# Weight loads put behind row stores, and the start of the first attention sequence in another order, in a fused FFN, mLSTM and FFN kernel

## The reference

```python
x = x + 0.5 * moe_ffn(layernorm(x))    # 8 experts, one per token: relu(x @ w1[e] + b1[e]) @ w2[e] + b2[e], times its softmax share
x = x + attn(layernorm(x))             # gated linear attention (mLSTM), below
x = x + 0.5 * moe_ffn(layernorm(x))    # same weights as the first

def attn(x):                           # 8 heads of 64; hidden width 512, inner width 256
    xn = layernorm(x) * g + b
    x_t, r_t = xn @ W_up_l.T + b_up_l, xn @ W_up_r.T + b_up_r
    x_c = silu(causal_conv4_over_features(x_t))
    q, k, skip = (x_c @ W.T + b for W_q, W_k / 8, W_skip);  v = x_t @ W_v.T + b_v
    i, f = softcap(x_c @ W_i.T + b_i), softcap(x_c @ W_f.T + b_f);  o = sigmoid(x_t @ W_o.T + b_o)
    # scan over the 512 tokens with a state c[h] (64 x 64), its normalizer n[h] and a running maximum m[h]
    h = o * scan(q, k, v, i, f)
    return (head_layernorm(h) + skip) * silu(r_t) @ W_down.T + b_down + x
```

## Time and profile before

| | |
|---|---|
| median of three runs | 426.08 us |
| profiled execution, in all | 429.1 us |
| its span, first to last instruction | 427.3 us |
| TensorE busy | 375.8 us (88%) |
| VectorE busy | 316.3 us (74%) |
| ScalarE busy | 236.5 us (55%) |
| GpSimd busy | 122.1 us (29%) |
| mean granted clock of TensorE | 0.946 |

### The profile page before, as it was taken

How to read it: one execution, slowest core, us unless ns; L and a number is a source line. 1 busy time by engine, 2 the same in 40 slices (tenths; PEclk the granted TensorE clock), 3 DMA queues, 4 the chain that set the end, 5 groups by cost and what they waited for, 6 DMA issues and landing times.

```text
span 427.3 us, 11335 instructions
## 1 busy us (share of the span) xinstructions
PE 375.8 (88%) x3628; PEld 301.4 (71%) x3629; DVE 316.3 (74%) x1007; ACT 236.5 (55%) x634; POOL 122.1 (29%) x123
## 2 busy tenths in 40 slices
PE   8147999977999999999999999999989866879991
PEld 5117999723687787887878878778768733679990
DVE  7833777653658898878989788988789994658780
ACT  3734656611546767467684567655556912646550
POOL 2333543077001111103110120111031168334552
PEclk9566999996999999999999999999999989889997
DMA  7996223111799997876730000000002612323320
GB/s 171 392 316 237 68 71 59 38 43 44 151 179 188 187 176 184 180 181 153 185 92 0 0 0 0 0 0 0 2 2 60 228 62 83 117 69 90 98 67 1
DMA packets 57089, 44.57 MB, mean 104 GB/s; under 512 B 4063, under 2 KB 53857, under 8 KB 56673
## 3 DMA queue, kind: packets, MB, share of 16 engines
q1 hardware_dynamic: 54018, 38.14, 37.5%
q0 software_dynamic: 2752, 5.73, 4.8%
q10 hardware_dynamic: 288, 0.31, 0.4%
HBM read 17.98 MB, written 25.73 MB: 102 GB/s over the span
## 4 chain that ended last, share of the span: by engine, by line
PE 68%; ACT 9%; DVE 7%; issue 6%; DMA 4%; POOL 2%; another core or an unknown queue 1%; POOLq 0%; ACTq 0%; SPq 0%; DVEq 0%
PE bank L960 64%; ACT WVT L837 3%; DMA xn_rows<-XN 2%; POOL slots L531 2%; DMA XB<-xn_rows,IDX 1%; DVE ST L1508 1%; ACT XN L659 1%; PE bank L1086 1%; PE bank L1343 1%; ACT E L846 1%; ACT W1R L857 1%; DVE QS L2111 1%; PE bank L1244 1%; DMA XN<-slots 1%
## 5 line engine op out<-in xcount | busy, mean ns | idle before, releaser
L599 POOL TENSOR_TENSOR HS<-HS,MHALF 128x8 f32<-128x8 f32 x16 | 26.4, 1647 | 130.6 <-DVE HS L2161 130.6
L737 ACT ACTIVATE HT<-bank,W1R 128x128 f32<-128x128 f32 x138 | 40.6, 365 | 21.3 <-issue 11.0
L960 PE MATMUL bank<-XBT,W1R 128*128 128x128 f32 x368 | 51.9, 286 | 0.1
L960 PE MATMUL bank<-W,HT 128*128 x368 | 50.1, 280 | 0.5 <-issue 0.5
L960 PEld LDWEIGHTS bank<-XBT,W1R 128*128 128x128 f32 x368 | 47.2, 201 | 0.8 <-issue 0.4
L960 PEld LDWEIGHTS bank<-W,HT 128*128 128x128 f32 x368 | 46.1, 197 | 1.0 <-issue 0.7
L837 ACT ACTIVATE WVT<-bank,AC 128x128 f32<-128x128 f32 x128 | 36.5, 375 | 11.7 <-PE bank L960 11.3
L960 PE MATMUL bank<-MASKB,IDB 128*128 128x512 bf16 x111 | 35.7, 424 | 7.9 <-DVE CREDIT L1960 5.2
L801 ACT ACTIVATE QKT<-bank,COLS 128x512 f32<-128x512 f32 x32 | 22.0, 687 | 28.9 <-PE bank L960 28.9
L545 POOL DMA_INDIRECT XB<-xn_rows,IDX x23 | 22.6, 984 | 32.9 <-PE bank L1086 19.9
L584 POOL DMA_INDIRECT out<-YB,IDX x23 | 22.6, 983 | 25.8 <-DVE YB L1794 17.4
(11 more groups left out here) (377 smaller groups left out, 989.0 us busy)
## 6 DMA issues: line engine op xcount, KB each, us to landing
slots<-FILL SPq DMA_DIRECT2D x74, 258.0 KB
W<-w SPq DMA_DIRECT2D x2, 2048.0 KB, 12.3
XN<-slots SPq DMA_DIRECT2D x23, 129.0 KB
W<-w SPq DMA_DIRECT2D x1, 2064.0 KB, 7.9
y_rows<-YB SPq DMA_DIRECT2D x23, 64.0 KB
X<-x SPq DMA_DIRECT2D x4, 256.0 KB, 5.3
xn_rows<-XN SPq DMA_DIRECT2D x2, 512.0 KB, 8.8
XN<-X SPq DMA_DIRECT2D x1, 768.0 KB, 5.1
```

Of the source, the lines that this page charges most:

```text
L599: g.tensor_tensor(HS[:, 3, :], HS[:, 2, :], MHALF[:, 0:H], ALU.pow).then_inc(roots_ready, 1)
L737: ins = a.activation(HT[:, j % 2, c, :], bank[2 + j % 2][:, c * P:(c + 1) * P], ACT.Relu, bias=W1R[:, j % 2, F + c:F + c + 1])
L960: return t_.matmul(o, l, r, start=start, stop=stop, skip_group_check=True)
```

## The change

- **SP.** W1 waits for two quarters of X, not for four. W2 is loaded in two halves, one behind each store of `xn_rows`, and counted by a semaphore of its own (`w2_loaded`). The constants wait for the third transpose of a block. The attention weights are loaded one by one behind the y stores of blocks 0 to 6.
- **GpSimd.** After the first four gathers of y come both roots, and then the other twelve gathers; three of these twelve stood ahead of the roots.
- **ScalarE.** `cast_mask` moves from turn 1 of the blocks to the front of `split_weights`.
- **VectorE.** The setups after the first move back: softmax shares behind block 2, the others behind blocks 6, 8, ... 22. `folds_low` is taken apart: the low parts for W_up_r and W_v before `scale_norm`, the one for W_o behind it. `conv_low` now signals on `folds_split` too.
- **TensorE.** Ten products of ones are added between the ranks and the map. Before the first z, 8 + 9 products stand around the wait for the variance in place of 10 ahead of it and 7 behind the folds' wait. `head_z` and `head_x` wait only for `conv_low`; the wait for all low folds stands ahead of the v and o projections.

```diff
@@ SP
-            sp.wait_ge(x_loaded[3], 16)
+            sp.wait_ge(x_loaded[1], 16)
             sp.dma_start(W1[:, :, :], w1).then_inc(ffn_loaded, 16)
             sp.dma_start(B2[:, :, :], b2.partition_broadcast(P)).then_inc(ffn_loaded, 16)
-            sp.dma_start(W2[:, :, :, :], w2).then_inc(ffn_loaded, 16)
-            for lo, hi in GROUPS[0]:
+            for n, (lo, hi) in enumerate(GROUPS[0]):
                 sp.wait_ge(xn_ready[0], hi)
                 sp.dma_start(xn_rows[lo * P:hi * P, :].rearrange("(t p) d -> p t d", p=P), XN0[:, lo:hi, 0:D])\
                     .then_inc(rows_sent, 16)
+                half = slice(n * NE // 2, (n + 1) * NE // 2)
+                sp.dma_start(W2[:, half, :, :], w2[:, half, :, :]).then_inc(w2_loaded, 16)
+            sp.wait_ge(xbt_full[0], 3)
             sp.dma_start(COLS[:, :], colpack).then_inc(cols_loaded, 16)
...
+            store_block(0, 0)
+            sp.dma_start(WULT[:, :], wult).then_inc(folds_loaded, 16)
+            sp.dma_start(WURT[:, :], wurt).then_inc(folds_loaded, 16)
+            sp.dma_start(WIFT[:, :, :], wift).then_inc(folds_loaded, 16)
+            store_block(1, 1)
+            sp.dma_start(WVT[:, :, :], wvt).then_inc(folds_loaded, 16)
+            store_block(2, 2)
+            sp.dma_start(WOT[:, :, :], wot).then_inc(folds_loaded, 16)
...
+            store_block(6, 2)
+            sp.dma_start(WDT[:, :, :], wdt).then_inc(attn_loaded, 16)
@@ GpSimd, first_outputs
-                pool.wait_ge(fold_full, 4)
-                to_tokens(range(4, 7), y_loaded[4])
                 pool.wait_ge(cols_loaded, 48)
                 norms(0)
-                to_tokens(range(7, 8), y_loaded[4])
+                pool.wait_ge(fold_full, 4)
+                to_tokens(range(4, 8), y_loaded[4])
@@ ScalarE: out of turn 1 of the first FFN, and into split_weights
                 act.wait_ge(y_full[0], NBLK)
+                cast_mask()
                 act.wait_ge(attn_consts, 1)
@@ TensorE, first FFN
+                    for n in range(10):
+                        mm(bank[7][:, :], MASKB[:, 0:P], MASKB[:, :])
                     pe.wait_ge(high_ready, 2)
...
-                pe.wait_ge(ffn_loaded, 48)
-                if f == 1:
-                    pe.wait_ge(w2_loaded, 16)
+                pe.wait_ge(ffn_loaded, 32)
+                pe.wait_ge(w2_loaded, 48 if f else 32)
@@ TensorE, start of the attention
             spin(4, 0)
             pe.wait_ge(y_loaded[3], 16)
-            spin(10, 0)
+            spin(8, 0)
             pe.wait_ge(a_var, 1)
+            spin(9, 0)
             pe.wait_ge(folds_split, 1)
-            spin(7)
             head_z(0)
-            spin(3)
+            spin(3, 1)
             head_x(0)
+            pe.wait_ge(folds_split, 2)
             project(0, 0, "v")
@@ VectorE
-                        if k % 2 == 0 and k // 2 < len(setup):
-                            setup[k // 2]()
+                        if k == 2:
+                            setup[0]()
+                        elif k > 4 and k % 2 == 0:
+                            setup[k // 2 - 2]()
...
                 conv_low()
+                fold_low(WURL, WURH, 6)
+                fold_low(WVL, WVH, 7)
                 scale_norm(0)
-                folds_low()
+                fold_low(WOL, WOH, 4)
+                folds_done()
```

More of the change, by code:

```diff
@@ L429, in _, with store_block @@
                     .then_inc(rows_sent, 16)
+                half = slice(n * NE // 2, (n + 1) * NE // 2)
+                sp.dma_start(W2[:, half, :, :], w2[:, half, :, :]).then_inc(w2_loaded, 16)
+            def store_block(k, j):
+                sp.wait_ge(y_ready[0], k + 1)
+                sp.dma_start(y_rows[bass.ds(k * P, P), :], YB[:, j, :]).then_inc(y_sent[0][j], 16)
+            sp.wait_ge(xbt_full[0], 3)
             sp.dma_start(COLS[:, :], colpack).then_inc(cols_loaded, 16)
@@ L433, in _ @@
             sp.dma_start(K[:, FIRST:], consts[:, FIRST:KEPT]).then_inc(consts_loaded, 16)
[L434 to L438, removed]
-            def store_block(k, j):
-                sp.wait_ge(y_ready[0], k + 1)
-                sp.dma_start(y_rows[bass.ds(k * P, P), :], YB[:, j, :]).then_inc(y_sent[0][j], 16)
-            with sp.Fori(0, TAIL // RING) as n:
+            store_block(0, 0)
[6 more added lines that the diff above has]
+            sp.dma_start(WOT[:, :, :], wot).then_inc(folds_loaded, 16)
+            store_block(3, 3)
+            sp.dma_start(WQT[:, :, :], wqt).then_inc(attn_loaded, 16)
+            store_block(4, 0)
+            sp.dma_start(WKT[:, :, :], wkt).then_inc(attn_loaded, 16)
+            store_block(5, 1)
+            sp.dma_start(WSKT[:, :, :], wskt).then_inc(attn_loaded, 16)
+            store_block(6, 2)
+            sp.dma_start(WDT[:, :, :], wdt).then_inc(attn_loaded, 16)
+            store_block(7, 3)
+            with sp.Fori(2, TAIL // RING) as n:
                 for j in range(RING):
@@ L745, in turn @@
                         relu(k + 1, (j + 1) % RING)
-                    if f == 0 and isinstance(k, int) and k == 1:
-                        cast_mask()
                     if f == 1 and isinstance(k, int) and k + 3 < AHEAD:
@@ L1745, in first_route @@
                 dve.wait_ge(eid_ready[f], 1)
-                dve.wait_ge(ffn_loaded, 48)
+                dve.wait_ge(ffn_loaded, 32)
                 copy_w1(0, 0, 0)
@@ L1952, in conv_low, with fold_low, folds_done @@
                 step.settle()
[L1954 to L1958, removed]
+                v.memset(CREDIT[:, 9:10], 0.0).then_inc(folds_split, 1)
+            def fold_low(low, high, i):
+                dve.wait_ge(w_high, {6: 5, 7: 6, 4: 7}[i])
+                did(v.tensor_tensor(low[:, :], bank[i][:, :], high[:, :].bitcast(F32), ALU.subtract))
+            def folds_done():
                 step.settle()
```

## The result

The changed kernel took 423.91 us (median of 15 runs, 422.37 to 426.39) against 426.06 (15 runs) for the kernel before: ratio 0.995, 95% interval 0.9926 to 0.9975. Forecast was 413.0 with a range of 409.5 to 418.5. The sign was right, the size was not: 2.2 us came of 13.4. The profiled execution took 422.66 us, with a span of 420.7.

A forecast was written before the change was run, and what follows sets the result against it. The prediction took TensorE to bound the block loop, with the chain leaving it for gathers and the wait before z. It summed 6.2 + 1.2 + 0 + 6.0 = 13.4 us, from 426.08 to 413.0, range 409.5 to 418.5.

The forecast's parts named there:

- part 4: From the last block to the gates: earlier roots, z and x products gain 6.0 us, bounds 3.5 and 6.5.
- Everything after it keeps its spacing: Behind the first x bank's read, tanh, silu, 11 products and gates were to shift whole, keeping the 6.0 us gain.
- part 2: TensorE's clock in the first blocks: less time at half clock, gain 1.2 us, bounds 0 and 2.7.
- Part 1: First FFN until its blocks start: earlier stores and faster gathers gain 6.2 us, bounds 2.8 and 6.8.
- 2.7 us bound: Upper bound of the clock gain: the time lost while the first 5.36 us of the blocks run at 0.50.
- blocks run above 2.0 us: Sign in the first FFN's block loop that the forecast is wrong; blocks were expected to stay 1.90 us apart.
- Part 3: Weight loads beside the first FFN's blocks: forecast to cost 0, bounds 0 and 1.6 us.
- Slow gathers: Rival at the first gathers: they stay slow beside W2's last half, gain 10.0 us, time 416.1; chance 0.12.
- starved gathers: Rival at blocks 4 to 12: weight loads starve the block gathers, making the kernel slower, up to 430; chance 0.03.
- The clock did fall: Rival: the clock falls anyway in the first blocks and around z, gain 9.7 us, time 416.4; chance 0.13.

The follow-up runs named there:

- e1: An unchanged copy of the kernel before, measured and traced again: 426.35 us, ratio 0.997.
- e9: The changed kernel, with GpSimd waiting for the gates' products before the gathers of tiles 8 to 15: 422.49 us, ratio 0.990.
- e17: Changed kernel, only GpSimd reordered: block gathers 3 to 6 one a block; three token gathers ahead of the roots, five behind, four after the gates: 418.71 us, ratio 0.981.
- e13: As e9, but in the blocks GpSimd runs three gathers ahead of the transposes instead of four: 421.52 us, ratio 0.990.
- e10: As e9, with the weight loads, the tables and the setups that need them moved later in the blocks: 421.84 us, ratio 0.988.
- e16: As e3, with the block gathers three ahead instead of four: 421.7 us, ratio 0.990.
- e4: The kernel before with only the attention-start part of the change (GpSimd, folds, z, clock products): 430.59 us, ratio 1.008.
- e5: As e4, with GpSimd waiting for the gates' products before the gathers of tiles 8 to 15: 421.5 us, ratio 0.988.
- e8: The kernel before with one edit, GpSimd taking the roots ahead of the gathers of tiles 4 to 6: 429.19 us, ratio 1.007.
- e15: The changed kernel, each gather of tiles 4 to 15 waiting for the one before to land, no hold for the gates: 433.52 us, ratio 1.013.
- e11: As e5, with plain loads by SP in stored order in place of the gathers of tiles 8 to 15: 420.77 us, one run.
- e12: As e5, with sixteen small memsets filling GpSimd's wait for the gates: 425.45 us, one run.
- e3: The kernel before with only the first FFN's part of the change (SP, cast_mask, setups, ten added products): 422.38 us, ratio 0.989.
- e6: As e4, but with the gathers of tiles 4 to 6 ahead of the roots again: 426.77 us, ratio 0.999.
- e7: As e4, without the 4 + 7 clock products and the wait for the tanh table ahead of z: 425.98 us, ratio 1.000.

## Why the prediction was wrong, point by point

The step that failed is in part 4, "Everything after it keeps its spacing": the gates' tanh came 5.0 us behind the gates' products, and the clock behind the hole was 0.50. Most of the rest is the clock of part 2, forecast at +1.2 and measured at -0.4 with the blocks.

- **Part 1, stores and gathers: right.** Forecast 6.2, measured 5.9. The second store landed at 24.43 (23.6 forecast), the second gather took 2.5 us to its transpose (3.0), which stood at 28.73 (28.5). The two misses cancel in part, which is luck.
- **Part 2, the clock: the mechanism came, the gain didn't.** The clock was 1.00 from the first block, the whole of the 2.7 us bound. Yet from the copy of block 0's transpose to that of block 7's it is 14.7 us after and 14.0 before (13.4 in e1). The late copies sit there, and four blocks take 2.0 to 2.3 us, which is the sign I had named ("blocks run above 2.0 us"). What was forecast at +1.2 measured at -0.4 over all blocks. In the repeats the level wasn't kept: e9 had 0.61 from 30 to 32 us and e17 0.50, and their block 7 stood within 0.2 us of the changed kernel's. The Trainium skill ("TensorE: Matmul & The Clock Gate", What's actually happening) has the point of change free-running; the changed kernel and e9 are the same up to there and were granted 1.00 and 0.61, which agrees. Single traces speak for the late results: e13, with prompt ones, has block 7 at 42.05, 0.8 us ahead of e9 at about the same clock (0.64 and 0.50 from 30 to 34 us, against 0.61 and 0.54), while the changed kernel's full clock put it 0.2 ahead of e9. They don't explain all of it: e13 still takes the 14.0 us of before.
- **Part 3, weights beside the blocks: right, by e10.** Forecast 0. e10 takes them away from the first blocks, and its block 7 stands 0.35 us earlier. Where only three gathers ran ahead, they began to tell (e13, e16).
- **Part 4, last block to gates: right as far as its work was traced, wrong from there.** z and the x products came near the forecast (4.9 to 5.2 us of 6.0; nine products at the 0.23 us of the row end at 95.8 and not 95.6, a small slip of the sum). Then the gates moved 10.7 us forward, beside gathers that before ended ahead of them, and their results were held for 5.0 us; behind it another 1.3 went, about what the half clock costs there (1.2). Of this part's 6.0, the gates' tanh kept 0.3. Nor would the forecast have come without the delay: with the gathers held (e9) the kernel took 422.5 us, as the first sequence behind the gates then took 2.8 us longer than before. I had asked of the twelve gathers only when they land. That answer was right (VectorE's combination at 116.3 waits for nothing), but what they cost is what ran beside them.
- **The rivals.** Slow gathers and starved gathers didn't come. The clock did fall behind the gates, as an effect of the hole. None of the rivals had a mechanism at the gates, and nothing in the trace of before showed one: there the gathers are over before the first gates product, and the z and x products that do run beside them are read in time.
- **The sum.** 5.9 - 0.4 + 5.2 = 10.7 us had been won at the gates' products, and 4.6 remained at the second sequence. The medians show 2.2. That the profile of before stood above its median did matter, which the prediction had denied: against e1's trace 3.4 us remain, and the profiled execution of the changed kernel is itself 1.25 us under its median.

That back-to-back gathers hold up TensorE's results at the gates is shown by e4 against e5, by e8 and by the changed kernel against e15, and what isn't enough by e11 and e12. How they do it isn't: the gathers and TensorE share nothing that these traces record. Nor is it shown why the same run of gathers spares the z, x, v and o products just ahead, and whether the issue or the landing counts. Open too is most of what e9 and e17 lose behind the gates (46 us where e3 has 43.3). e5 against e11 shows that gathers behind the gates bring such a loss, but in e17 two gaps of TensorE, 1.25 us at 127.4 and 0.87 at 138.2, stand far behind the last gather.

## What to carry to other kernels

When work is pulled forward, list what it will newly run beside, on every engine, and not only whether its inputs are ready and its outputs land in time. A wait of a reader far behind the recorded end of its product, with "remote" as its releaser, was here the mark of DMAs that GpSimd was issuing, and holding those back costs one line to try. It isn't free: the gathers held in e5 cost 1.8 us further on, against e11. Where two halves of a change each look good, time them alone: here one gained 1.1% and the other lost 0.8%. And trace the kernel before twice: of its first profile, 1.2 us weren't in the second.

## What the runs showed of the hardware

- A run of row gathers that GpSimd issues 1.25 us apart delayed the gates' results by 3.2 to 5.1 us in four kernels (after, e4, e6, e7). Not every result beside such a run is late: z and the x products were read within 0.4 us in all of them. The gates' products were reported within 0.1 us with no gather being issued (e5, e9, e15, e17), beside 248 GB/s of plain transfers (e11) and beside memsets (e12).
- A gather's issue, 0.95 us, took 1.59 to 1.97 us where it met a VectorE operation on 128x1024 floats (1.23 us): XC at 97.12 and XCL at 105.51 after, XCL at 110.01 in e4 and at 104.61 in e5. The Trainium skill ("GPSIMD Engine Reference", 1. Specifications) says that GpSimd shares its ways into SBUF with VectorE and that operations with two SBUF inputs contend; these rows agree.
- A matmul's record may lie 5 us ahead of the moment at which its result can be read, with the granted clock at 1.00 throughout.
